# Row tile transposes at the head of TensorE's step, beside the gated product's transposes, in a mixture-of-experts tile stage

## What is computed

```python
x = L0_attn_x
x = _layernorm(x + _L0_attn_ref(x, ...), axis=-1)
# experts, for the tokens xf = x.reshape(-1, 256)
probs = jax.nn.softmax(xf @ gate_w.T, axis=-1)
top_w, top_idx = jax.lax.top_k(probs, 4)
h1 = jnp.einsum('td,ehd->teh', xf, w1)
h3 = jnp.einsum('td,ehd->teh', xf, w3)
act = jax.nn.silu(h1) * h3
eout = jnp.einsum('teh,edh->ted', act, w2)
moe_out = jnp.einsum('ted,te->td', eout, combine)
shared = jax.nn.silu(xf @ sw1.T) * (xf @ sw3.T) @ sw2.T
x = _layernorm(x + moe_out + shared, axis=-1)
```

## Time and profile before

| | us |
|---|---|
| median of 3 runs | 585.02 |
| lowest and highest | 583.97, 585.84 |
| span of the profiled execution | 582.6 |

### The profile page before, as it was taken

How to read it: one execution, slowest core, us unless ns; L and a number is a source line. 1 busy time by engine, 2 the same in 40 slices (tenths; PEclk the granted TensorE clock), 3 DMA queues, 4 the chain that set the end, 5 groups by cost and what they waited for, 6 DMA issues and landing times.

```text
span 582.6 us, 11203 instructions
## 1 busy us (share of the span) xinstructions
PE 530.6 (91%) x3204; PEld 466.6 (80%) x3205; DVE 462.5 (79%) x1061; ACT 373.1 (64%) x769; POOL 366.0 (63%) x337
## 2 busy tenths in 40 slices
PE   4999999999999999999897399999999998988654
PEld 2687888888888887888765399999999898988643
DVE  5859798989989899898889866555556788886954
ACT  4726475856668476683709247777777776776652
POOL 0081406686776867778675777776676676766740
PEclk9899999999999999999896789999999999999977
DMA  7629321473434334322992966665567999999985
GB/s 248 207 52 385 106 73 36 163 227 116 124 99 155 101 111 130 99 104 81 297 333 85 289 215 194 211 192 188 182 199 242 344 298 349 315 294 342 366 276 207
DMA packets 72375, 117.10 MB, mean 201 GB/s; under 512 B 10006, under 2 KB 54103, under 8 KB 72026
## 3 DMA queue, kind: packets, MB, share of 16 engines
q1 hardware_dynamic: 43114, 62.38, 34.6%
q0 software_dynamic: 21136, 45.76, 22.9%
q10 hardware_dynamic: 8080, 8.41, 4.1%
HBM read 72.87 MB, written 47.87 MB: 207 GB/s over the span
## 4 chain that ended last, share of the span: by engine, by line
PE 67%; DVE 15%; DMA 7%; issue 4%; ACT 3%; POOL 1%; SPq 1%; POOLq 0%; ACTq 0%; DVEq 0%
PE bank L785 10%; PE bank L876 8%; PE bank L971 7%; PE bank L973 7%; PE bank L972 7%; PE bank L763 6%; PE bank L1021 4%; PE bank L933 4%; PE bank L817 4%; DMA xt<-expert_rows 4%; PE bank L994 2%; DMA token_parts<-ty,goes 2%; PE bank L942 2%; PE bank L925 2%; DVE onehot L1579 2%
## 5 line engine op out<-in xcount | busy, mean ns | idle before, releaser
L732 POOL DMA_INDIRECT token_parts<-ty,goes x144 | 143.1, 994 | 59.5 <-issue 31.7
L706 POOL DMA_INDIRECT expert_rows<-row,slot x112 | 120.7, 1078 | 55.3 <-issue 29.1
L971 PE MATMUL bank<-w_hi,xtT_hi 128*128 x288 | 87.5, 304 | 8.7 <-DVE xtT_lo L1688 8.7
L973 PE MATMUL bank<-w_hi,xtT_lo 128*128 x288 | 81.4, 283 | 0.0
L972 PE MATMUL bank<-w_lo,xtT_hi 128*128 x288 | 81.2, 282 | 0.0
L971 PEld LDWEIGHTS bank<-w_hi,xtT_hi 128*128 128x128 f32 x288 | 54.7, 190 | 9.0 <-issue 9.0
L876 PE MATMUL bank<-mats,Y 128*128 128x256 f32 x256 | 58.6, 388 | 1.9 <-DVE Y L1445 1.9
L1241 ACT ACTIVATE ty<-bank,xt 128x256 f32<-128x256 f32 x144 | 60.3, 470 | 0.1
L763 PE MATMUL bank<-zt,mats 128*128 128x256 f32 x256 | 58.0, 382 | 0.8 <-DVE slot L1585 0.8
L1688 DVE TENSOR_TENSOR xtT_lo<-bank,xtT_hi 128x512 fp32r<-128x512 f32 x72 | 49.4, 687 | 11.6 <-ACT xtT_hi L1230 11.6
L876 PEld LDWEIGHTS bank<-mats,Y 128*128 128x128 f32 x256 | 49.1, 194 | 9.2 <-DVE Y L1445 1.6
(11 more groups left out here) (211 smaller groups left out, 1369.1 us busy)
## 6 DMA issues: line engine op xcount, KB each, us to landing
xt<-expert_rows SPq DMA_DIRECT2D x144, 129.0 KB, 2.8
row<-token_parts SPq DMA_DIRECT2D x21, 640.0 KB, 7.1
row_last<-token_parts SPq DMA_DIRECT2D x7, 640.0 KB
xT<-in_xT SPq DMA_DIRECT2D x8, 512.0 KB, 4.0
xtok<-in_x SPq DMA_DIRECT2D x8, 512.0 KB, 3.8
w_hi<-in_w POOLq DMA_DIRECT2D x1, 4096.0 KB, 17.3
w_lo<-in_w SPq DMA_DIRECT2D x4, 1024.0 KB, 11.6
xT_hi<-in_xT POOLq DMA_DIRECT2D x7, 512.0 KB, 4.6
```

The lines of the kernel that those rows point to most:

```text
L706: pool.indirect_dma_start(out=rows_d, out_offset=bass.IndirectOffsetOnAxis(ap=slot[q][:, n:n + 1], axis=0), in_=src[:, n // TOPK, n % TOPK ...
L732: pool.indirect_dma_start(out=parts_d, out_offset=bass.IndirectOffsetOnAxis(ap=goes[:, q_ * UNROLL + u:q_ * UNROLL + u + 1].bitcast(U32), ...
L971: te_.matmul(ps, x_hi, w_hi, start=first, stop=False)
L973: return te_.matmul(ps, x_lo, w_hi, start=False, stop=last)
```

## The change

TensorE's step has X first, then A, H and Y. X and A stand next to each other. The bank that X writes is read by ScalarE and VectorE for the pair two turns back; before, H's wait for `t_xlo` stood ahead of X and covered that. X now has a wait of its own for the same count (the pair's number less one). No other engine's program is changed.

```diff
             def turn(g, j, q, h):
                 if j == 0:
                     load_experts(g)
+                pair = back(g, j, q, h, 0)
+                if pair:
+
+                    after(pe_e, t_xlo, pair[4] - 1)
+                    for a in range(2):
+                        at = q * UNROLL + 2 * j + a
+                        pe_e.wait_ge(ld_xt[at], 16 * (h + 1))
+                        for c in range(DC):
+                            mm = te_.transpose(bank[j % 2][:, (a * DC + c) * P:(a * DC + c + 1) * P], xt[:, at, c * P:(c + 1) * P],
+                                               ident[:, :])
+                    mm.then_inc(t_xT, 1)
                 pair = back(g, j, q, h, AT_A)
                 if pair:
 
...
                     mm.then_inc(t_h, 1)
                     if isinstance(k, int) and k == 0:
                         shared_out(B, 6)
-                pair = back(g, j, q, h, 0)
-                if pair:
-
-                    for a in range(2):
-                        at = q * UNROLL + 2 * j + a
-                        pe_e.wait_ge(ld_xt[at], 16 * (h + 1))
-                        for c in range(DC):
-                            mm = te_.transpose(bank[j % 2][:, (a * DC + c) * P:(a * DC + c + 1) * P], xt[:, at, c * P:(c + 1) * P],
-                                               ident[:, :])
-                    mm.then_inc(t_xT, 1)
                 pair = back(g, j, q, h, AT_Y)
                 if pair:
```

## The result

The changed kernel takes 588.76 us (median of 4 runs, 588.17 to 593.60) beside 584.50 us (581.74 to 585.84) for the kernel before: a ratio of 1.0093, 95% interval 1.0049 to 1.0136, about 4.3 us slower. In a later comparison, with the kernels of experiment g1, it was 590.32 us beside 583.47, ratio 1.0109, interval 1.0062 to 1.0156. The forecast was 589.0.

What follows compares the result with a forecast made beforehand. TensorE was taken to bound the first stretch, and loads filling the DMA engines the second. Terms 0 + 0 + 0.5 + 0.3 + 3.7 - 0.5 = 4.0 us on 585.0 gave 589.0 us, range 585.2 to 594.0.

Steps and rivals of the forecast that it cites:

- (1): TensorE, each turn of the tile stage: one fewer change between transposes and products gives 0 us, at most 0.7 us either way.
- (2): A, H and followers start 0.44 us later, Y's copy-out on ScalarE 0.33 us later; cost in the first stretch 0.
- (3): New wait at the turn's head for VectorE's low part: 0.5 us in the second stretch, between 0 and 1.8 us.
- (4): Row loads' cover falls from 5.5 to 3.5 us; late loads cost 0.3 us in the first stretch, 3.7 in the second.
- the sign that I had named: Second stretch, X of turn 39 to X of turn 71, grows beyond 98.9 us by 2 to 6 us.
- The lower one: Second stretch, row loads: landing times stay where they are, so only the last late load counts, costing 1.7 us.
- The upper one: Second stretch, row loads: latencies stay, turns last 3.27 us instead of 3.09, and the stretch grows by 5.7 us.
- (5): Second stretch: unexplained late starts of A, 3.5 us in all, shrink; between 0 and 3.5 us return, taken as 0.5.
- latency falls as turns lengthen: Rival: DMA engines pace the second stretch, TensorE's wait only moves to the head; 585.0 to 586.5 us, chance 0.20.
- Full feedback: Rival: second-stretch latencies stay and every turn lasts 3.27 us, 10.3 us slower, about 595 us; fallen clock may add; chance 0.12.

Runs made afterwards that it cites:

- g1: The changed kernel run again, unchanged, in a later comparison with the kernel before: 590.32 us, ratio 1.0109.
- h2: The changed kernel with the 640 KB part loads cut to 16 columns, part of the output left out: 577.27 us, ratio 0.9878 to the kernel before.
- h1: The kernel before with the 640 KB part loads cut to 16 columns, part of the output left out: 574.05 us, ratio 0.9821 to the kernel before.
- g2: The kernel before with X moved behind Y on TensorE, grouped with the next turn's A, ScalarE's order left alone: 584.59 us, ratio 1.0027.
- Groups f: Comparison of both kernels unchanged and both with part loads cut to 16 columns: kernel before 628.79 us, changed kernel 630.61 us, ratio 1.0028.

## Why the prediction held, step by step

The sum was +4.0 us; medians gave +4.3 in the first comparison and +6.9 in the second, spans +4.6. That +4.0 and +4.3 are so near is in part luck: the row loads, forecast at +4.0, measured +7.5 in the profile (1.0 and 6.5), and parts of the span that the forecast left alone took 3.0 us off.

(1) Grouping, taken as 0 with 0.7 us either way. It gives a little. The timeline of the changed kernel, turns 18 and 19 (start, length, engine, line):

```profile
379.98 0.60 PE L994 MATMUL bank<-ident,xt 128*128 128x128 f32 x4
...
380.31 0.19 ACT L1240 COPY goes<-xt 128x2 int32<-128x2 int32 x1
...
380.41 0.83 ACT L1242 ACTIVATE ty<-bank,xt 128x256 f32<-128x256 f32 x2
380.42 0.38 PE L1005 MATMUL bank<-ident,ta 128*128 128x128 f32 x2
...
381.42 6.32 SPq L551 DMA_DIRECT2D xt<-expert_rows  x6
...
382.25 0.39 ACT L1224 ACTIVATE tsl<-bank 128x256 f32<-128x256 f32 x1 [0.74 <-PE bank L973]
...
382.53 0.58 ACT L1231 CAST xtT_hi<-bank 128x512 fp32r<-128x512 f32 x1
...
382.76 0.60 PE L994 MATMUL bank<-ident,xt 128*128 128x128 f32 x4
```

From X to X are 382.76 - 379.98 = 2.78 us, against 2.80 us in the earlier trace rows. Over many undisturbed turns it is 2.780 us (22 turns of h2 from 424.33 to 485.49) against 2.794 (37 turns of h1 from 425.75 to 529.11): 0.014 us per turn, 1.0 us for 72. My reading error per turn was too small by a third, because I had judged it by single starts printed to 0.01 us.

(2) A and H later, copy-out 0.33 us later, cost 0. Half right. Silu is 0.42 us later in the turn (2.27 us from the head, 1.85 in the earlier trace rows), as predicted. But the copy-out starts 0.24 to 0.33 us after the next turn's head, against 0.20 in the earlier trace rows, so it is 0.04 to 0.13 us later only: the cast used to wait for X and now doesn't, and takes up the delay. SP issues 1.44 us after the head in both kernels (381.42 - 379.98; 381.30 - 379.86).

(3) The head wait for VectorE's low part, 0.5 us. In the first profile no matmul waited for it from 440 to 546 us, and one weight load did, 2.6 us. In g1 it was two, 3.7 us in all, and again no matmul. The 2.6 us are the same stop as the longest wait for a row load, 2.5 us before X of turn 68: the low part that this X needs was done at 529.1 us, its first load landed at 533.9, and X began at 534.0. I count the term as 0.

(4) Row loads, 0.3 + 3.7 us. The mechanism, loads that land after their use, was right and the size too small. The cover fell from 5.5 to 3.8 us (second load asked for at about 381.94, second half of X at 385.76), not to 3.5, since the copy-out is hardly later. Even so the first stretch lost more than its 0.6 us shows: with the shorter beat it should have gained 31 x 0.014 = 0.4, so late loads cost 1.0 us there and 2.1 in g1. I had read the slowest landing as 3.4 us from the line of matched loads (9 of 66) and allowed 1 at the most; over all 66 the slowest took 4.4. The second stretch lost 6.5 us, and 5.8 in g1, with the beat's gain of 0.4 us already taken off; the sign that I had named was 2 to 6.

My two ends both failed. The lower one, 1.7 us, rested on landings that stay where they are in time. They don't: SP's loads wait for the copy-out of a turn that waits itself, and the DMA engines fall from 0.94 to 0.90 busy. It also took 7.76 us in the earlier trace rows for a wait of TensorE; that is the load's own time, and TensorE waited 1.0 us before those matmuls. The upper one took every turn to last as long as the median load allows, (4.9 + 4.9) / 3 = 3.27 us. The stretch had 105.33 / 32 = 3.29 us per turn, but that agreement is luck. With the measured cover and the median over all loads the sum is (8.34 - 3.8 + 4.4) / 3 = 2.98, and only 17 of the 32 turns are longer than 2.9 us (10 before). What grew is seen from X of turn 39 to X of turn 71, before, changed and g1 (columns as above):

```profile
440.62:539.45 98.83, 92.34 (x770) 89.43 (x769) 78.71 (x198) 73.65 (x205) 69.34 (x69) 1.00 0.94 317
438.88:544.21 105.33, 96.14 (x771) 92.09 (x769) 80.68 (x199) 69.84 (x205) 69.12 (x69) 0.97 0.91 298
439.42:544.09 104.67, 94.60 (x771) 90.55 (x770) 81.12 (x198) 69.44 (x205) 69.08 (x69) 0.98 0.89 300
```

TensorE's idle time (length less busy time) grew from 6.5 to 9.2 us, and in g1 to 10.1. The other 3.8 us, and 2.3 in g1, are the same matmuls taking longer. The rule of the Trainium skill, page "DMA: Bandwidth & Descriptors", section "Issuing engines are not separate DMA queues", is not refuted by that: the three busiest queues of the kernel before hold 68, 21 and 4% of the same 16 engines from 440 to 541 us. But the engines were not always full, and my step from the one to the other was what failed.

Most of that longer busy time fits the clock, which I had put into a rival. After 1.84 us of waiting:

```profile
483.85 1.08 PE L994 MATMUL bank<-ident,xt 128*128 128x128 f32 x4 [1.84 <-DMA xt<-expert_rows]
...
485.80 0.41 PE L971 MATMUL bank<-w_hi,xtT_hi 128*128 x1
...
486.02 0.41 PE L972 MATMUL bank<-w_lo,xtT_hi 128*128 x1
```

the products follow each other at 0.22 us instead of 0.12: the granted clock is at 1.2 GHz from 484.3 to 487.7 us and a second time from 535.5 to 538.9, which are the two windows at 0.83 above. Each time 3.4 us at half pace put off 1.7 us of work, 3.4 us in all at most, less where the next load would have been late anyway. So up to half of the loss of the stretch is the clock. In h2, where no wait for a row load was over 0.6 us, the clock is 1.00 from 440 to 541 us. g1 had one such fall in this stretch (0.83 from 450 to 460 us), behind waits of 0.5 and 1.7 us within one turn; yet a wait of 1.79 us at 492.06 left it at 1.00 (485 to 500 us). So the length of one wait does not tell by itself whether the clock falls. The Trainium skill's rule on transposes ("TensorE: Matmul & The Clock Gate", Part 4: they do not count as busy for the clock as products do) did no harm: with 0.66 us of transposes in one piece per turn the first stretch stays at 1.00, in the changed kernel and in g2. No run here has transposes alone, so the rule itself is not tested.

(5) A's holes, 0.5 us back. They nearly went: 3.5 us in the earlier trace rows, 0.2 now, 0.6 in g1. But they came back into turns that wait for loads, as said, and can't be found in the length of the stretch.

Two parts of the span that I had left alone cancelled the excess. The start-up is 1.2 us shorter than the 28.58 us of before, in both profiles of the changed kernel (27.41 and 27.44 us). That can't be put down to the change: h1 has the old order, its cut loads come only later, and its start-up is 28.73 - 1.65 = 27.08 us. The granted clock rises at 339.1 us in before, and at 337.6, 336.8 and 336.4 in the changed kernel, g1 and h1, so the first profile of before seems to have been late there. The end, from the head of turn 71, is 1.8 us shorter (1.1 in g1). With the part loads cut it is 0.5 us longer (45.27 against 44.81). That fits an end that waits for part loads, which get ahead while TensorE waits in the tile stage; beyond this pair of profiles it is argued, not shown.

Of the rivals, "latency falls as turns lengthen" was right about the latency, by 0.3 to 0.4 us of the median, and wrong about the time. "Full feedback" had the fallen clock, which came, and turns that all wait, which did not; its 10.3 us were too much.

## What to carry to other kernels

Before a consumer is moved to the head of a turn, take the time from the issue of its load to its use, subtract the move, and hold the rest against the slow landings of the busiest stretch, not against the mean. Take the landings of all loads, not a median over the few that a view could match. If a load is issued by the result of a turn that can itself wait for a load, a wait can feed the next one; and waits of TensorE can cost its clock on top, here up to half of the loss. Saving 0.014 us per turn on TensorE brought nothing where the DMA engines were 0.95 busy: g2's second stretch stayed at 99 us.

## What the runs showed of the hardware that I had not expected

- Placing all transposes of a turn in one group, at the head or at the end, shortens an undisturbed turn from 2.794 to 2.780 us.
- The granted clock fell to 1.2 GHz for 3.4 us at a time behind waits of 1.84 and 2.5 us (changed kernel) and of 0.5 and 1.7 us in one turn (g1); a wait of 1.79 us in g1, and those of the kernel before, up to 1.2 us, left it at 2.4 GHz.
- The same kernel took 583 to 585 us in three comparisons and 625 to 629 in two. In the slower ones ScalarE stood still for 2 to 4 us about every 7 us, half of the time with no releaser in the trace, at a DMA share of 0.50. Groups f (slower) and g (not) bear the same chip number on record, 10, so the chip alone does not explain it. The cause is open.
- Even with the part loads cut, single row loads of 129 KB took up to 4.6 us (h1) and 4.5 (h2) at a DMA share of 0.62 to 0.67, beside a median over all loads of 2.3 to 2.5.
